# Two-layer graph network: the node stages rebuilt, Q and R split after P, indices loaded for four chunks

## What is computed

```python
h = relu(layernorm(x))
# layer 0, for every edge
e  = relu([h[src], h[dst], edge_attr] @ We1 + be1)        # 32 wide
m  = relu(e @ We2 + be2)                                  # 128 wide
h2 = relu([h[dst], m] @ Wn1 + bn1)                        # 64 wide
x  = x + h + segment_sum(relu(h2 @ Wn2 + bn2), dst)
h  = relu(layernorm(x))
# layer 1, for every edge
msg = (h[src] @ W[etype] + b[etype]) * weight
x   = x + relu(segment_sum(msg, dst))
```

## Time and profile before

| what | value |
|---|---|
| three runs | 8136.67, 8141.24, 8145.61 us; median 8141.24 |
| profiled execution, span (first to last instruction) | 8149.0 us |
| what lies outside that span in the profiled execution | not shown; its span alone is known |
| PE busy | 6825.6 us, 84% |
| POOL busy | 6074.5 us, 75% |
| DVE busy | 3995.9 us, 49% |
| ACT busy | 1919.9 us, 24% |
| first gather issued / last gather of layer 0 | 145.69 / 4082.33 us |
| first / last gather of layer 1 | 4166.52 / 8098.87 us |

### The profile page before, as it was taken

One profiled execution on the slowest core, in us unless ns is written; L12 is line 12 of the kernel. 1 busy time (PEld: TensorE's weight loads), 2 busy tenths in 40 slices (PEclk: granted clock), 3 DMA queues, 4 the chain that ended last, 5 costly groups with the idle time before them and its releaser, 6 DMA issues.

```text
span 8149.0 us, 187072 instructions
## 1 busy us (share of the span) xinstructions
PE 6825.6 (84%) x52884; PEld 5276.0 (65%) x52884; DVE 3995.9 (49%) x13480; ACT 1919.9 (24%) x4919; POOL 6074.5 (75%) x6335
## 2 busy tenths in 40 slices
PE   5999999999999999999967777777778877777777
PEld 4666666666666666666646666666666666666665
DVE  7333333333333333333365555555555556555554
ACT  2333333333333333333330000000000000000001
POOL 5777777777777777777757777777777777777776
PEclk7999999999999999999979888888888888988898
DMA  6333333333333333333322222222222222222222
GB/s 141 82 83 82 81 83 82 83 82 83 82 83 82 82 83 82 83 83 82 82 61 53 53 53 53 53 53 52 53 53 53 53 52 53 52 53 53 53 53 72
DMA packets 797549, 566.94 MB, mean 70 GB/s; under 512 B 481443, under 2 KB 671019, under 8 KB 797292
## 3 DMA queue, kind: packets, MB, share of 16 engines
q0 software_dynamic: 200192, 256.65, 14.6%
q1 hardware_dynamic: 597340, 310.10, 14.5%
HBM read 544.45 MB, written 21.68 MB: 69 GB/s over the span
## 4 chain that ended last, share of the span: by engine, by line
PE 32%; issue 24%; POOL 21%; DMA 20%; DVE 1%; POOLq 1%; SPq 0%; ACT 0%; DVEq 0%; ACTq 0%
PE bank L1130 19%; POOL shared L549 17%; DMA shared<-p_tab,idx 11%; DMA rows_place<-h_tab,idx 6%; PE bank L1143 5%; POOL rows_place L549 4%; PE bank L1132 3%; DMA idx<-in_src_t 2%; PE bank L1054 2%; PE bank L1145 1%; PE bank L1061 1%; PE bank L1080 0%; DMA x_in<-in_x 0%; PE bank L1071 0%; DVE stats L744 0%
## 5 line engine op out<-in xcount | busy, mean ns | idle before, releaser
L549 POOL DMA_INDIRECT shared<-p_tab,idx x3128 | 2984.1, 954 | 959.8 <-issue 826.7
L549 POOL DMA_INDIRECT rows_place<-h_tab,idx x3128 | 2978.3, 952 | 964.3 <-issue 804.4
L1130 PE MATMUL bank<-shared,rows_place 128*128 128x256 f32 x6256 | 1842.2, 446 | 860.4 <-issue 748.1
L1130 PEld LDWEIGHTS bank<-shared,rows_place 128*128 128x128 f32 x6256 | 1296.4, 218 | 1126.6 <-issue 782.8
L959 DVE TENSOR_SCALAR shared<-iota_key,key,w_f 128x256 f32<-128x256 f32 x3128 | 1139.1, 425 | 745.3 <-PE bank L1132 633.1
L704 ACT ACTIVATE x_in<-bank 128x256 f32<-128x256 f32 x782 | 300.8, 385 | 3591.9 <-PE bank L1132 3264.7
L1061 PE MATMUL bank<-h_sb,w_tile 128*128 128x128 f32 x6256 | 907.7, 288 | 22.3 <-DVE h_sb L870 0.8
L1061 PEld LDWEIGHTS bank<-h_sb,w_tile 128*128 128x128 f32 x6256 | 758.5, 191 | 232.4 <-DVE h_sb L870 232.1
L1080 PE MATMUL bank<-wn_half,h_sb 128*128 128x128 f32 x6256 | 890.3, 285 | 0.0
L870 DVE TENSOR_SCALAR h_sb<-bank 128x128 f32<-128x128 f32 x782 | 228.2, 292 | 1315.8 <-PE bank L1054 1294.3
L1143 PE MATMUL bank<-x_in,w_rel_sb 128*128 128x64 f32 x6256 | 862.8, 296 | 0.0
(11 more groups left out here) (105 smaller groups left out, 5379.0 us busy)
## 6 DMA issues: line engine op xcount, KB each, us to landing
rows_place<-in_dst_c SPq DMA_DIRECT2D x782, 192.0 KB
shared<-in_edge_cols SPq DMA_DIRECT2D x782, 128.0 KB
shared<-p_tab,idx POOLq DMA_INDIRECT x3128
rows_place<-h_tab,idx POOLq DMA_INDIRECT x3128
idx<-in_src_t SPq DMA_DIRECT2D x1564, 2.0 KB
qr_w<-qr_tab SPq DMA_DIRECT2D x782, 18.0 KB
x_in<-in_x SPq DMA_DIRECT2D x14, 448.0 KB, 4.7
h_tab<-x_in SPq DMA_DIRECT2D x14, 448.0 KB, 3.0
```

The source lines that it names most:

```text
L549: pool.indirect_dma_start(out=rows_of[s][:, t, :], out_offset=None, in_=table, in_offset=bass.IndirectOffsetOnAxis(ap=idx[s][:, t:t + 1], ...
L1130: pe.matmul(bank[s][:, 0:RW], rows[s][:, t, :], hot_rel[s % 2][:, t, :], start=(t == 0), stop=(t == TC - 1))
```

## The change

Five things are changed together.

1. **x lands in place.** SP issues all 14 loads of x at the start, straight into `res`; `x_in` is gone. Its weights, constants and `dst_f` follow; edge types and weights are loaded only after layer 0 (their place, `late`, holds the split's parts until then).
2. **Normalisation on ACT.** DVE makes rstd and shift = -mean * rstd for a group (7 columns), and ACT writes h = relu(rstd * x + shift) in seven activations. Both node stages do so; the DVE passes L766, L770 and the POOL pass L584 are gone. The biases be1 and bn1 go into the edge loop: `relu_h1` adds be1 and takes the maximum in one DVE instruction, `relu_h2` uses ACT's bias. `add_bias` becomes a plain copy into `agg`, which now holds the products of all 14 groups.
3. **The split of Q and R is put off past P.** First all groups are projected and P is stored; then seven parts of 14 tiles are split, conversions on ACT and subtractions on DVE, with three places for the parts. POOL waits only for P before its first gather.
4. **agg is transposed where it lies.** No staging copy. In the second node stage PE transposes four tiles of a group; the other three it sums on top of x in PSUM (a product of `res` with the identity, then three of `agg`), and ACT copies that half back. `agg` is cleared by POOL group by group. In the last stage DVE does all groups.
5. **Indices by four chunks.** One load brings the indices of four chunks (8 KB), in two places; that of the next four is issued at the fourth chunk's turn.

The node stages are written out group by group instead of looping. Core of the diff:

```diff
@@ sync, first stage
-            load_x(Group(0, 0))
-            load_x(Group(0, 1))
+            for g in range(2):
+                load_x(g)
             for there, source in w_node_parts:
                 sp.dma_start(there, source).then_inc(node_consts_landed, 16)
+            for g in range(2, 5):
+                load_x(g)
             sp.dma_start(dst_rows[:, :, :], dst_c.rearrange("(q k) e -> q k e", q=QP)).then_inc(dst_landed, 16)
-                sp.wait_ge(lo_done, k.n + 1)
-                hold(sp)
-                for t, part in enumerate((qr_hi, qr_mid, qr_lo)):
-                    sp.dma_start(node_rows(qr_tab[t], k.i), part[b][:, :, :]).then_inc(parts_stored[b], 16)
+            for g in range(5, NG):
+                load_x(g)
+            load_idx(0, 0, idx_landed)
+            sp.wait_ge(zeroed, 5)
+            for there, source in edge_consts:
+                sp.dma_start(there, source).then_inc(consts_landed, 16)
             sp.dma_start(dst_f[:, :].bitcast(i32), dst_t).then_inc(dstf_landed, 16)
+            for g in range(NG):
+                sp.wait_ge(pqr_copied, 2 * g + 2)
+                sp.dma_start(node_rows(p_tab, g), group(pqr, g)[:, :, 0:H1]).then_inc(p_stored, 16)
+            for q in range(NPART):
+                sp.wait_ge(lo_done, q + 1)
+                for t in range(3):
+                    sp.dma_start(node_rows(qr_tab[t], q * (PT // TPG), PT // TPG), qr_part[q % PB][t]).then_inc(parts_stored[q % PB], 16)
@@ sync, layer 0
-                    sp.dma_start(idx[s][:, :], src_t[:, ds(c.i * TC, TC)]).then_inc(idx_landed[s], 16)
+                    if s == SL - 1:
+                        load_idx(c.quad + 1, 1 - k, idx_landed)
+            parts_all_stored(sp)
             with sp.Fori(0, passes) as m:
                 layer0_pass(m)
+            load_idx(0, 0, idx1_landed)
+            sp.dma_start(et_key.bitcast(i32), etype_t).then_inc(ids_landed, 16)
+            sp.dma_start(w_f, weight_t).then_inc(weight_landed, 16)
@@ gpsimd
-            for b in range(2):
-                pool.wait_ge(p_stored[b], 16 * (NG // 2))
-            pool.wait_ge(parts_stored[0], 48 * (NG // 2))
+            for g in range(NG):
+                pool.wait_ge(h_done, g + 1)
+                pool.tensor_tensor(group(res, g), h[g % HB], group(res, g), ALU.add).then_inc(res_done, 1)
+            pool.wait_ge(p_stored, 16 * NG)
+            for g in range(NG):
+                pool.wait_ge(agg_transposed, 2 * g + 2)
+                pool.memset(agg[:, g * TPG * P:(g + 1) * TPG * P], 0.0).then_inc(agg_cleared, 1)
@@ scalar
+            def normalise(n, g):
+                act.wait_ge(shift_done, n + 1)
+                for j in range(TPG):
+                    at = g * TPG + j
+                    ins = act.activation(h[g % HB][:, j, :], res[:, at, :], ACT.Relu, bias=shift[:, at:at + 1],
+                                         scale=rstd[:, at:at + 1])
+                ins.then_inc(h_done, 1)
+            hi(0)
+            for q in range(NPART):
+                if q + 1 < NPART:
+                    hi(q + 1)
+                mid(q)
+            act.activation(agg[:, NPAD // 2:], zero_col[:, :].broadcast_to([P, NPAD // 2]), ACT.Copy).then_inc(half_cleared, 1)
-                act.activation(agg_group[b][:, :], agg[:, ds(g * (TPG * P), TPG * P)], ACT.Copy).then_inc(agg_staged[b], 1)
@@ vector
+            remainder(0)
+            for q in range(NPART):
+                if q + 1 < NPART:
+                    remainder(q + 1)
+                low(q)
+            dve.wait_ge(p_stored, 16 * NG)
+            dve.wait_ge(lo_done, NPART)
+            dve.memset(agg[:, 0:NPAD // 2], 0.0).then_inc(agg_added, 1)
@@ vector, first node stage and edge loop
+            def copy_pqr(g):
+                for a, (t0, t1) in enumerate(HALVES):
+                    dve.wait_ge(pqr_ready, 2 * g + a + 1)
+                    dve.tensor_copy(group(pqr, g)[:, t0:t1, :], tiles_of(banks_of(2 * g + 1, 4)[a], t1 - t0)).then_inc(pqr_copied, 1)
-                dve.tensor_scalar_max(h1_sb[:, :], ps_h1[:, 0:P], 0.0).then_inc(h1_done, 1)
+                dve.tensor_scalar(h1_sb[:, :], ps_h1[:, 0:P], be1_col[:, 0:1], 0.0, ALU.add, ALU.max).then_inc(h1_done, 1)
@@ tensor, second node stage
+                for j in range(t0, t1):
+                    at = (g * TPG + j) * P
+                    ins = pe.transpose(first[:, (j - t0) * P:(j - t0 + 1) * P], agg[:, at:at + P], ident[:, :])
+                pe.matmul(second[:, 0:(t3 - t2) * P], ident[:, :], group(res, g)[:, t2:t3, :].rearrange("p j d -> p (j d)"),
+                          start=True, stop=False)
+                for j in range(t2, t3):
+                    at = (g * TPG + j) * P
+                    ins = pe.matmul(second[:, (j - t2) * P:(j - t2 + 1) * P], agg[:, at:at + P], ident[:, :],
+                                    start=False, stop=(j == t3 - 1))
```

More of the change, by code:

```diff
@@ L111, in gnn_two_layers, with in_shared @@
+        HB = 4
+        h_place = sb("h_place", [P, HB, TPG, D])
+        h = [h_place[:, k, :, :] for k in range(HB)]
+        shared = sb("shared", [P, SL * TC * (EA + H1) + 2 * CH])
+        hT = [sb("hT", [P, TPG * P]), shared[:, 0:TPG * P]]
+        stats = sb("stats", [P, 2, TPG, 6])
+        mv = sb("mv", [P, NTILE, 2])
+        std = sb("std", [P, NTILE])
+        rstd = sb("rstd", [P, NTILE])
+        shift = sb("shift", [P, NTILE])
         taken = 0
-        def in_agg(n, parts=P):
+        def in_shared(n):
@@ L811, in step @@
+            for g in range(NG + 3):
+                if g < NG:
+                    dve.wait_ge(x_landed[g], 16)
+                    statistics(g, g)
+                if 1 <= g <= NG:
+                    scales(g - 1, g - 1)
+                if g >= 3:
+                    copy_pqr(g - 3)
+                if g == 1:
                     ramps()
-                    dve.wait_ge(node_consts_landed, 16 * N_NODE_CONST)
-                if group and isinstance(group.i, int) and group.i == 1:
+                if g == RANGE_AT:
@@ L1037, in _ @@
+            pe.wait_ge(node_consts_landed, 16 * N_NODE_CONST)
+            for g in range(NG + 1):
+                if g < NG:
+                    transpose_h(g)
+                if g >= 1:
+                    project_nodes(g - 1)
+            pe.wait_ge(pqr_copied, 2 * NG)
             pe.wait_ge(consts_landed, 16 * N_CONST)
```

635 lines of the change are left out of this document (268 added, 367 removed).

## The result

The changed kernel is slower: 8178.0 us (median of 4 runs, 8176.3 to 8186.0) against 8142.7 for the kernel before on the same chip, ratio 1.0044 (95% interval 1.003 to 1.0058). The loss is 0.4%, small but clear of the interval. The prediction was 8101 in a range of 8086 to 8128, with 0.07 for slower. It was wrong in the sign.

What follows compares the result with a forecast made beforehand. POOL issuing 6256 gathers without a stall was taken to bound 97% of the span. Gains of 27 + 10 + 3 = 40 us made 8149.0 into 8109, less 8 for the profiled execution 8101; range 8086 to 8128.

Steps and rivals of the forecast that it cites:

- Indices, biases: Edge loops: fewer index loads and biases in instructions of the same size give 0, bounds 10 us either way.
- The rival for slower: Gathers: POOL's longer loop and new index layout make each cost more; at 12 ns, 8176 us; chance 0.07.
- First node stage: Ahead of layer 0: faster groups and later Q and R stores gain 27 us, bounds 13 and 39.
- forecast 39: First node stage: storing the parts, 7.2 MB at 185 GB/s, needs 39 us of DMA time.
- sign 85 to 100: Start of layer 0: the first gather comes at 85 to 100 us if the forecast holds.
- the sum for one group: First node stage, per group: DVE 3.7 us, ACT 3.8, PE 3.0 or 5.1; taken as 4.3.
- the index load that I had said couldn't be late: Edge loop: SP issues the next four chunks' indices well before POOL finishes the current chunk; no cost.
- The pause: Start of layer 0: POOL waits 15 to 30 us for `sum_h1` after its first gathers.
- Second node stage: Between the layers: faster groups and an earlier index load among the terms; gain 10 us, bounds 4 and 14.
- the 1.65 I booked for it: Second node stage: clearing agg leaves DVE, so 1.65 us of idle before POOL's second gather goes.
- Last stage: After the last gather: store issue bounds it; dropping the staging copy and engine alternation gains 3 us, bounds 0 and 5.
- in a rival, 5: Both layers: part of the gathers' cost goes with SP's loads, 10 us more over 6256 gathers, 8091; chance 0.08.

Runs made afterwards that it cites:

- chip D, alone: Kernel before with only the index loads by four chunks, in both layers; 8153.7 us, 0.9977 of the kernel before on its chip.
- with it on chip E: The complete changed kernel run again on another chip, be1 column included; 8131.6 us, 0.9973 of the kernel before there.
- without it on chip D: Changed kernel with be1 left out of layer 0's ReLU, a plain maximum again; 8111.5 us, 0.993 of the kernel before on its chip.
- both instructions moved away: Changed kernel with DVE's `hot` and `hotT` of the next chunk ahead of the ReLU instead of behind it; 8089.9 us, 0.9932 of the kernel before.
- the exchanged one: Kernel before with `hotT` made ahead of `hot` instead of behind it; 8187.1 us, 1.0015 of the unedited kernel before.
- Two kernels with the changed kernel's layer 1: Changed kernel with be1 left out (8111.5 us, 0.993 of the kernel before), and with `hotT` ahead of `hot` (8155.1 us, 0.9981).

## Why the prediction was wrong

**The step that failed** is "Indices, biases", which I set at 0 with bounds of ±10 us. POOL indeed never waited for indices, and the biases do ride in instructions of the same size. But I asked only what the loads and the column cost, not what they move. The loads' going locks layer 0's phase (chip D, alone), and the column's 0.06 us comes on top (third gather 1.003 us with it on chip E, 0.966 without it on chip D, where the rows land equally early). Together they made 73 us on the chip of the result. How much of it is the column's there was not run; as an estimate from the law, 0.06 us less of `hotT` behind the third gather's start would give back 0.06 x 778 = 46 us.

**The rival for slower** said that each gather costs more, 12 ns, 8176 us. The time is right and the reason isn't, so the hit is luck: the indices' layout and the shape of POOL's loop did nothing (chip E, both instructions moved away: 944 to 948 ns with both unchanged). 24 ns came in layer 0 alone, all in the third gathers. It had been in the rows: a gather of 1.07 or 1.12 us, a `hotT` of 0.54 beside one. I put this down to neighbours in general. Sorting the gathers of the trace before by `hotT`'s start would have given the law, and with it a chance well over 0.07 for a change that touches DVE's or SP's part of the chunk.

**First node stage**: 14.7 instead of 27. First gather at 94.90 (forecast 90, sign 85 to 100). The last copy of P, Q and R ended at 90.6, not 84; the first part was ready at 95.0, not 89; the stores kept their rate (39.02 us, forecast 39). The first `sum_h1` ended at 144.8, not 138. The granted clock was 0.75 to 0.84 between 20 and 100 us. That is 6.8 us. Two terms of the sum for one group were mis-sized. The seven activations take 2.80 us, not 2.15: the row that I took them from has a scale column and no bias column. And DVE's shift of 7 columns, 0.17 us long, took 1.90 to 2.04 us in 6 of 14 groups, because POOL's addition `res` had begun ahead of it; both end together, and ACT waits, 8 us in all:

```profile
77.26 2.08 POOL L525 TENSOR_TENSOR res<-h_place,res 128x896 f32<-128x896 f32 x1 [3.20 <-ACT h_place L560]
77.42 1.95 DVE L703 SCALAR_TENSOR_TENSOR shift<-mv,rstd 128x7 f32<-128x7 f32 x1
79.48 2.80 ACT L560 ACTIVATE h_place<-res,shift,rstd 128x128 f32<-128x128 f32 x7 [1.25 <-DVE shift L703]
```

It is the same contest as in layer 0, the other way round. 5 us more were lost to the index load that I had said couldn't be late: at the start of layer 0 all slots are free, SP is behind its stores, and the load for the fifth chunk stands behind the fourth chunk's (149.69). The third `sum_h1` ended at 158.04, which frees the seventh chunk's slot; POOL, held up before, came to it at 163.31. The pause was 37 us instead of 15 to 30.

**Second node stage**: 12.3 instead of 10, stretch 70.9 (forecast 73). From the sixth group on one takes 3.26 us instead of 3.6, and it is ACT that sets the pace, not DVE as I had it (0.50 for the half copied back, 0.32 for the root, 2.82 for the activations, without a pause). The wait before the second gather stayed (1.86 for 1.95), so the 1.65 I booked for it didn't come; the faster pace made up for it.

**Last stage**: 10.5 instead of 3. The stores did bound it (19.68 us of issue, 24.14 before), but I took their pace as fixed; they start 14 us behind the last gather instead of 16, and each takes 1.4 instead of 1.72 us.

**Layer 1**: 8.4 where I had 0 and, in a rival, 5. The index loads don't explain it: on chip D the kernel before took 3942.0 us for layer 1 with loads by four chunks, and 3941.3 with loads chunk by chunk (the exchanged one). Two kernels with the changed kernel's layer 1 took 3933.2 and 3948.4 there, so 8.4 us is within what the same code strays by.

## What to carry over

Where one engine issues back to back, write down when each instruction of the engine that shares something with it starts, relative to the issuing one; a tuned loop can sit beside a cliff of 0.05 us. An edit that costs nothing by itself (a load less on a queue, an operand more) moves that phase, and a loop whose waits feed back on themselves either strays or locks. Put the shared-resource instructions where the other engine has just begun, with a margin larger than the spread, and time the result on more than one chip.

## What the runs showed of the hardware

- A gather issued by GpSimd waits for some VectorE instructions that began ahead of its start, until they end: 944 ns become up to 1220 (`hotT`, 0.54 us, begun over 0.13 us ahead) or 1437 on average (0.74 us, begun 0.15 ahead). A `hotT` that begins 0.40 to 0.65 us behind a gather's start grows instead (0.54 to at most 0.78 us). Unhindered gathers take 942 to 947 ns everywhere.
- The other way round, a VectorE instruction of 0.17 us took 1.9 to 2.0 us beside an addition of GpSimd (2.1 us) that had begun 0.07 to 0.21 us ahead of it (6 of 6 cases in the changed kernel's first stage).
- Rows of a gather land in 1.1 us, but in 2.0 when a 192 KB load was issued 0.4 to 1.0 us ahead of the gather's end (trace of the kernel before).
- The same kernel took 8142, 8154, 8171 and 11677 to 11910 us on different chips, and the change made 1.0044, 0.9973 and 0.8877 of it.
